# Moving the preparation of the weights from VectorE to ScalarE in the statistics stage, and measuring the second chunk in halves

## The reference

```python
def _gn(v, G=32, eps=1e-5):                      # statistics over all 512 x 512 positions
    g = v.reshape(B_, H_, W_, G, C_ // G)
    m = jnp.mean(g, axis=(1, 2, 4), keepdims=True)
    s = jnp.var(g, axis=(1, 2, 4), keepdims=True)
    return ((g - m) / jnp.sqrt(s + eps)).reshape(v.shape)

x = x + _L0_conv_ref(_gn(x), ...)   # layer norm, five 64x64 products, a mask m_i*m_j, sigmoid gates, einsum, layer norm, product
x = x + _L1_conv_ref(_gn(x), ...)   # a product in the lowest 12x12 Fourier modes
```

## Time and profile before

| What | Value |
|---|---|
| median of 3 runs | 3029.33 us (3028.93 to 3033.02) |
| the profiled execution | 3029.29 us, span 3027.5 us |
| PE busy over the span | 2510.4 us (83%) |
| DVE busy | 2207.5 us (73%) |
| ACT busy | 1372.8 us (45%) |
| POOL busy | 1020.9 us (34%) |
| mean granted clock of PE | 0.946 of full speed |

### The profile page before, as it was taken

How to read it: one execution, slowest core, us unless ns; L and a number is a source line. 1 busy time by engine, 2 the same in 40 slices (tenths; PEclk the granted TensorE clock), 3 DMA queues, 4 the chain that set the end, 5 groups by cost and what they waited for, 6 DMA issues and landing times. The chain is left out here.

```text
span 3027.5 us, 40932 instructions
## 1 busy us (share of the span) xinstructions
PE 2510.4 (83%) x12694; PEld 1864.6 (62%) x12694; DVE 2207.5 (73%) x3463; ACT 1372.8 (45%) x1778; POOL 1020.9 (34%) x1042
## 2 busy tenths in 40 slices
PE   0008999889889979999999992989988988789775
PEld 0005666556556658888888881556655655588664
DVE  5998888778778748888888885766766766226453
ACT  0006888778778857666766671212211221100000
POOL 1018888778778800000000000444444444300000
PEclk9999999999999989999999996999999999769988
DMA  9845999788779767777777773999999999749999
GB/s 375 341 188 192 341 337 336 287 307 314 284 294 336 285 256 280 275 282 285 281 277 280 284 263 129 389 379 379 377 372 371 380 386 364 247 163 393 418 419 406
DMA packets 260650, 950.26 MB, mean 314 GB/s; under 512 B 31153, under 2 KB 31665, under 8 KB 260146
## 3 DMA queue, kind: packets, MB, share of 16 engines
q1 hardware_dynamic: 226160, 877.25, 76.7%
q10 hardware_dynamic: 34370, 71.54, 6.1%
HBM read 540.83 MB, written 407.90 MB: 313 GB/s over the span
## 5 line engine op out<-in xcount | busy, mean ns | idle before, releaser
L1104 POOL TENSOR_TENSOR fi_square_sum<-fi_square_sum,fi_square 128x1024 f32<-128x1024 f32 x128 | 302.7, 2365 | 429.0 <-ACT fi_square L1075 429.0
L780 PE MATMUL ct_acc_ps<-ct_l_hi,ct_r_hi 128*128 128x512 f32 x1024 | 404.3, 395 | 20.6 <-ACT ct_l_hi L794 20.6
L652 DVE SCALAR_TENSOR_TENSOR pj_lr<-pj_v_ps,layer_b_val,pj_sig 128x1024 f32<-128x1024 f32 x256 | 328.8, 1284 | 121.7 <-ACT pj_sig L589 118.4
L1075 ACT ACTIVATE fi_square<-fi_x 128x1024 f32<-128x1024 f32 x128 | 135.4, 1057 | 600.5 <-DVE fi_x L1132 590.9
L781 PE MATMUL ct_acc_ps<-ct_l_lo,ct_r_hi 128*128 128x512 f32 x1024 | 404.2, 395 | 0.0
L782 PE MATMUL ct_acc_ps<-ct_l_hi,ct_r_lo 128*128 128x512 f32 x1024 | 404.1, 395 | 0.0
L1031 PE MATMUL fi_y_ps<-fi_scaled,layer_w_bd 128*128 128x512 f32 x512 | 282.1, 634 | 71.1 <-DVE fi_scaled L1115 70.9
L490 POOL TENSOR_TENSOR front_ring<-front_ring,layer_gn_shift 128x512 f32<-128x512 f32 x256 | 333.5, 1304 | 5.5 <-DVE front_ring L618 5.5
L1115 DVE TENSOR_TENSOR fi_scaled<-fi_m,fi_s_ps 128x512 f32<-128x512 f32 x256 | 174.0, 680 | 190.5 <-DMA fi_m<-mixed_d 162.5
L589 ACT ACTIVATE pj_sig<-pj_g_ps,layer_b_gate 128x1024 f32<-128x1024 f32 x256 | 285.5, 1115 | 43.0 <-PE pj_g_ps L555 40.5
L1302 PE MATMUL la_ps_ps<-la_col,la_inv_cols 128*128 128x256 f32 x1024 | 243.3, 400 | 46.5 <-DVE la_early L1372 28.0
(11 more groups left out here) (183 smaller groups left out, 5035.8 us busy)
## 6 DMA issues: line engine op xcount, KB each, us to landing
lr_d<-pj_lr SPq DMA_DIRECT2D x128, 1024.0 KB, 5.8
gate_d<-pj_gout SPq DMA_DIRECT2D x128, 512.0 KB, 6.8
ct_l<-lr_d SPq DMA_DIRECT2D x64, 1024.0 KB, 7.1
ct_r<-lr_d SPq DMA_DIRECT2D x64, 1024.0 KB, 9.0
mixed_d<-ct_o SPq DMA_DIRECT2D x64, 1024.0 KB, 4.9
fi_m<-mixed_d SPq DMA_DIRECT2D x128, 512.0 KB, 14.1
fi_g<-gate_d SPq DMA_DIRECT2D x128, 512.0 KB, 12.9
fi_x<-in_x SPq DMA_DIRECT2D x32, 2048.0 KB, 9.1
```

Source lines behind the costliest of these rows:

```text
L652: dve.scalar_tensor_tensor(out=out[:, :, RG * (m % 2):RG * (m % 2) + RG], in0=v_ps[:, :].rearrange("p (q i) -> p q i", i=RG), scalar=keep. ...
L780: pe.matmul(bank, high, l_hi[b][:, :, k, :], start=(k == 0), stop=False)
L1104: pool.tensor_tensor(square_sum[:, :, :], square_sum[:, :, :], square[:, :, :], ALU.add).then_inc(sum_done, 1)
```

## The change

Three things are done in `prepare`.

1. Chunk 1 is measured in halves too (`HALVED` = chunks 0, 1 and 7). `SPLIT` goes from 4 to 6 and `SLOTS` from 10 to 11, so the instructions that combine the slots read 704 columns for 640.
2. ACT does the arithmetic on the weights and masks, behind its transfers, with `Copy` (and a scale) or `Identity` (and a bias). On DVE only the conversion of the masks, `mask_sq` and the three low parts stay.
3. DVE's order changes: `statistics` 0, 1 and 2, then the masks, then 3, 4 and 5, then the low parts, then 6 and 7.

```diff
-SPLIT = 4
-SLOTS = SPLIT + NCHUNK - 2
+HALVED = (0, 1, NCHUNK - 1)
+SPLIT = 2 * len(HALVED)
+SLOTS = SPLIT + NCHUNK - len(HALVED)
...
         def _(act):
             for dst, src in loads:
                 act.dma_start(dst, src).then_inc(loaded, DMA)
+            link = chained(act, act_step)
+            def copy(dst, src, scale=1.0):
+                return act.activation(dst, src, ACT.Copy, scale=scale)
+            def add(dst, src, bias):
+                return act.activation(dst, src, ACT.Identity, bias=bias)
+            act.wait_ge(loaded, DMA * len(loads))
+            act.wait_ge(pool_set, 7)
+            copy(ow_scaled[:, :], ow[:, :], onw[:, 0:1])
+            copy(w_scaled[:, :, :], w_raw[:, :, :], nw[:, 0:1]).then_inc(scaled_ready, 1)
...
+            last.then_inc(raw_ready, 1)
+            copy(keep.minus[:, :], keep.ident[:, :], -1.0)
+            act.wait_ge(products, 1)
...
+            link(copy(mask_wide[:, :], m_ps[:, :]))
+            for i, (w_high, w_low) in enumerate((keep.w_val, keep.w_gate, keep.w_og)):
+                copy(w_high[:, :], w_full[:, i, :]).then_inc(w_split, 1)
+            by_parity = mask_wide[:, :].rearrange("p (j e) -> p e j", e=2)
+            act.wait_ge(mask_ready, 1)
+            for k in range(WT):
+                copy(keep.mask_row[:, :, k, :], by_parity, maskf_col[:, k:k + 1])
             act.wait_ge(root_in, 1)
...
-            for i in range(2):
+            for i in range(3):
                 statistics(i)
             dve.wait_ge(loaded, DMA * len(loads))
...
             dve.tensor_copy(maskf_row[:, :], mask_row[:, :]).then_inc(row_ready, 1)
...
-            for i in range(2, NCHUNK):
+            for i in range(3, NCHUNK - 2):
+                statistics(i)
+            for i, (w_high, w_low) in enumerate((keep.w_val, keep.w_gate, keep.w_og)):
+                dve.wait_ge(w_split, i + 1)
+                dve.tensor_tensor(w_low[:, :], w_full[:, i, :], w_high[:, :], ALU.subtract)
+            for i in range(NCHUNK - 2, NCHUNK):
                 statistics(i)
```

More of the change, by code:

```diff
@@ L188, in prepare @@
         root_ready = t.sem("root_ready")
+        act_step = t.sem("act_step")
+        mask_ready = t.sem("mask_ready")
+        w_split = t.sem("w_split")
         loads = []
@@ L246, in _ @@
                 act.dma_start(dst, src).then_inc(loaded, DMA)
+            link = chained(act, act_step)
[7 more added lines that the diff above has]
+            copy(w_scaled[:, :, :], w_raw[:, :, :], nw[:, 0:1]).then_inc(scaled_ready, 1)
+            for h in range(2):
+                rows = slice(h * C, (h + 1) * C)
+                copy(ow_bd[rows, h * C:(h + 1) * C], ow[rows, :])
+                last = copy(w_raw_bd[rows, :, h * C:(h + 1) * C], w_raw[rows, :, :])
+            last.then_inc(raw_ready, 1)
+            copy(keep.minus[:, :], keep.ident[:, :], -1.0)
+            act.wait_ge(products, 1)
+            for h in range(2):
+                rows = slice(h * C, (h + 1) * C)
+                copy(w_full[rows, 2, h * C:(h + 1) * C], w_ps[rows, 4, :])
+                copy(keep.w2_bd[rows, h * C:(h + 1) * C], ow_ps[rows, :])
+            for h in range(2):
+                rows = slice(h * C, (h + 1) * C)
+                copy(w_full[:, 0, rows], w_ps[:, 2 * h, :])
+                copy(w_full[:, 1, rows], w_ps[:, 2 * h + 1, :])
+                add(keep.b_val[rows, :], b_ps[rows, 2 * h:2 * h + 1], bias_in[rows, 2 * h:2 * h + 1])
+                add(keep.b_gate[rows, :], b_ps[rows, 2 * h + 1:2 * h + 2], bias_in[rows, 2 * h + 1:2 * h + 2])
+            add(keep.b_out[:, :], b_ps[:, 4:5], bias_in[:, 4:5])
+            add(keep.c_col[:, :], c_ps[:, :], out_b[:, 0:1])
+            link(copy(mask_wide[:, :], m_ps[:, :]))
[5 more added lines that the diff above has]
+                copy(keep.mask_row[:, :, k, :], by_parity, maskf_col[:, k:k + 1])
             act.wait_ge(root_in, 1)
@@ L274, in statistics @@
                 b, done = i % 2, DMA * (i // 2) + DMA
-                if i in (0, NCHUNK - 1):
+                if i in HALVED:
                     for h in range(2):
                         dve.wait_ge(x_loaded[b][h], done)
-                        at = 6 * (h if i == 0 else 2 + h)
+                        at = 6 * (2 * HALVED.index(i) + h)
                         tok = slice(STATS_T // 2 * h, STATS_T // 2 * h + STATS_T // 2)
@@ L284, in statistics @@
                         dve.wait_ge(x_loaded[b][h], done)
-                    at = 6 * (SPLIT + i - 1)
+                    at = 6 * (SPLIT + i - 2)
                     for g in range(G):
@@ L300, in _ @@
-            last.then_inc(raw_ready, 1)
             dve.tensor_copy(maskf_row[:, :], mask_row[:, :]).then_inc(row_ready, 1)
-            link(dve.tensor_copy(maskf_col[:, :], mask_col[:, :]))
+            dve.tensor_copy(maskf_col[:, :], mask_col[:, :]).then_inc(mask_ready, 1)
+            dve.wait_ge(mask_ready, 1)
             dve.tensor_tensor(keep.mask_sq[:, :], maskf_col[:, :], maskf_col[:, :], ALU.mult)
[L304 to L315, removed]
@@ L322, in _ @@
                 dve.tensor_tensor(w_low[:, :], w_full[:, i, :], w_high[:, :], ALU.subtract)
-            by_parity = mask_wide[:, :].rearrange("p (j e) -> p e j", e=2)
-            for k in range(WT):
-                dve.tensor_scalar(keep.mask_row[:, :, k, :], by_parity, maskf_col[:, k:k + 1], None, ALU.mult)
-            for i in range(2, NCHUNK):
+            for i in range(NCHUNK - 2, NCHUNK):
                 statistics(i)
```

5 lines of the change are left out of this document (removed).

## The result

The changed kernel takes 3010.38 us (median of 17 runs, 3008.52 to 3018.52). The kernel before, run beside it 17 times, takes 3026.27 us (3016.47 to 3033.86). The ratio is 0.9955, with a 95% interval of 0.9944 to 0.9965: 10.6 to 16.9 us faster. The forecast was 3018.2 us in a range of 3014 to 3023, and 11.1 us faster.

What follows compares the result with a forecast made beforehand. It took the statistics stage to be bound by one chain of chunk transfers and DVE measurements through the even buffer. 11.5 us gained less 0.4 for combining gave 3029.3 - 11.1 = 3018.2 us, range 3014 to 3023.

Steps and rivals of the forecast that it cites:

- The chain through the even buffer: Statistics stage: chunks 2, 4, 6 sent for, landed and measured in turn, then chunk 7; starting earlier, it ends 11.5 us sooner.
- The combination: End of the statistics stage on DVE: 704 columns for 640 and longer reductions cost 0.4 us, within 0 to 0.5.
- The halves "next to nothing": Statistics stage: measuring chunk 1 in halves gains next to nothing, costing 1.9 us of DVE inside a wait of 9.7 us.
- ACT's work at no cost: Statistics stage: the weight arithmetic moved to ACT ends by 110 us, 42 us before DVE needs it, and costs nothing.
- DVE's code, "I expect 0": Loop of project: DVE's code ahead grows by one instruction; the second wait comes one instruction earlier, ends unchanged: 0 us.
- The second wait: DVE's 3.6 us idle at each of four branches in project; rival that it goes away: 14.4 us gained, chance 0.04.
- the transfers keep part of it: Rival, statistics stage: chunks 4 and 6 take 25 us from issue, not 23.3; 3.4 us lost, 3021.6 us, chance 0.07.
- PE's clock gives it back: Rival: the moved work meets two more falls of PE's clock, so 3028.2 us, no change; chance 0.06.
- The slower rival, ACT's code: ACT's code moves by 31 instructions; waits of 9.1 us at four branches, behind DVE's, add 36.4 us: 3054.6 us, chance 0.03.
- the level and the range: Whole kernel: starting time 3029.3 us; 3017 to 3021 with the spread of the runs, 3014 to 3023 holding the first two cases.

Runs made afterwards that it cites:

- e1: The changed kernel without the halves of chunk 1 (only chunks 0 and 7 in halves): 2997.67 us, ratio 0.9916 to the kernel before.
- e5: The kernel before with 31 small activations more on ACT ahead of the root: 3022.16 us beside 3022.52 us of the kernel before.
- e9: The changed kernel with 20 small activations more on ACT and nothing on DVE: 3015.14 us, ratio 0.9969 to the kernel before.
- e2: The kernel before with only chunk 1 measured in halves, the weights staying on DVE: 2967.81 us, ratio 0.9816 to the kernel before.
- e4: The changed kernel with five small memsets more on DVE ahead of the combination: 2997.91 us, ratio 0.9918 to the kernel before.
- before again: The kernel before, unchanged, run once more for a second trace: statistics 215.0, project 883.9, rest 1919.5 us.
- changed again: The changed kernel, unchanged, run once more for a second trace and ratio: 3013.53 us beside 3025.51 us, ratio 0.9953.

## Why the prediction was right and wrong, point by point

**The chain through the even buffer: right.** Chunk 2 at 70.60 (forecast 70.4), chunk 4 at 113.39 (112.8), chunk 6 at 155.52 (155.2), the end of measuring at 195.46 (195.2). The round trips took 23.69 us (89.70 to 113.39) and 23.04, for 23.3 taken.

**The combination: right.** From the end of measuring to `project` 8.67 us for 8.23, 0.44 more for 0.4. The row of 704 columns takes 1.07 for 0.99.

**The halves "next to nothing": near.** 1.4 us gross, 0.9 net (e1), through chunk 5, which the working followed for the changed kernel but not for the kernel without halves.

**ACT's work at no cost: right**, with more cover than taken.

**DVE's code, "I expect 0": right.** The second wait moved by one instruction, from behind the third to behind the second `bn_stats`, and project stayed within its spread.

**The rivals "the transfers keep part of it" and "PE's clock gives it back": neither came.** The round trips are above. The mean granted clock is 0.947 for 0.946 before, and what stands behind the statistics stage kept its length, as shown below.

**The slower rival, ACT's code: its mechanism came, its price did not.** ACT got 27.8 us of waits, and they lie under DVE's; e5 and e9 show them at nothing. The condition that the prediction named, "behind DVE's, not under them", did not hold. Its reason, that ACT waits for PE at that place anyway, holds only while DVE waits. In e2, where DVE doesn't, that wait is gone; waits of e2 in 525 to 570 us, at the first branch:

```profile
ACT pj_high L580 <- PE pj_x_ps L533: 2.5, 14, 0.3
```

Its longest is 0.3 us for 10.7. With DVE's waits gone, ACT's cost 29 us of project (e4, 869.9 for 841).

**The step that failed: the level and the range, "with the spread of the runs, 3017 to 3021" and 3014 to 3023.** They took three runs of 3028.93 to 3033.02 for the level of the kernel. Over 17 runs, these three among them, it is 3026.27, with 3016.47 to 3033.86; in the three later series it is 3021.8, 3022.5 and 3025.5. That is 3.0 us of the 7.8 by which the time was missed: the term of the sum that was mis-sized is its start, 3029.3, and with 3026.3 in its place the forecast would have been 3015.2. The other 4.8 is the difference of the medians, 15.9, less the 11.1 forecast; in the traces the change is worth 10.8. Does the change do more than the statistics stage? Three traces have the old stage and DVE's waits (before, before again, e5) and three the new one (changed, changed again, e9). What stands behind the statistics stage, project and rest, is 2812.6, 2803.4 and 2805.8 us in the first, mean 2807.2, and 2805.4, 2808.9 and 2807.0 in the second, mean 2807.1. So the traces show no gain behind the stage, and a spread of 9 us for one and the same kernel; 10.8 us lie within both intervals of the ratio, and e9, the changed kernel but for 20 small activations, has 0.9969, which is 9.4 us. That the surplus of the medians is chance is thus what fits, but runs without a trace can't be taken apart, and a surplus of 2 or 3 us stays possible. The range left no room for either: one trace and three runs did not show how wide a kernel's times lie.

**What the prediction walked past.** It read four times 9.1 us of DVE's idle time at the branches and priced only the second wait, at 14.4 us with a chance of 0.04. Six memsets were worth 38.6 us, more than three times the 10.8 us of the change. Against the traces of before, project is 43 to 47 us shorter for 34 to 36 us of waits: behind each wait PE also runs at the lower level of its clock for some microseconds. Windows of 5 us of before, behind the wait at the first branch, and of e2, at the same place without a wait (the third number from the end is the granted clock):

```profile
560.00:565.00 5.00, 4.24 (x14) 2.73 (x14) 4.57 (x12) 1.09 (x2) 4.61 (x10) 0.50 0.00 0
```

```profile
545.00:550.00 5.00, 5.00 (x34) 3.22 (x30) 3.99 (x9) 4.53 (x7) 4.56 (x8) 1.00 1.02 418
```

## What to carry to other kernels

When several edits aim at one wait, ask for the floor of that wait first: here it was a landing at 70.6 us, each edit alone came within 2.5 us of it, and both together brought hardly more than one. An idle time in front of a loop's first instruction with no releaser is worth a test of its own before anything else: move the loop by a few instructions on that engine and look whether it goes. Any edit that changes the count of instructions ahead of a loop such as these, of 276 and 308 instructions, can bring or take such waits, so a comparison of two kernels should name the loops' places beside the times.

## What the runs showed of the hardware

A taken branch cost DVE 4.6 to 5.8 us and, where 5 or 6 instructions of the pass lay ahead of instruction 963 and not 36, another 3.5 to 4.0 us; it cost ACT 5.9 to 7.2 us; and with the loop in other places nothing. DVE's loop of 308 instructions waits from 927, 957 and 958, and not from 963, 988 and 1109. ACT's loop of 276 waits from 560 and 561, and not from 529, 580 and 785. The Trainium skill, "Runtime: NRT & Kernel Launch", section "Instruction fetch mechanics", says that most engines hold two blocks of 256 instructions of their code and that a taken branch to code outside them must fetch. With an edge of a block at 963 on DVE, the loops that wait touch three blocks and those that don't touch two; on ACT all five places fit an edge between 562 and 579, with the same result. The traces agree with the page; the durations and the places of the edges are theirs alone. By the page's 256 a loop of up to 257 instructions would never touch more than two blocks, and a longer one would or wouldn't by its place; the shorter case no run here tests.
